# Gate and up products of the first two shared chunks issued in the attention's program, and the PSUM banks of the experts dealt out anew

## The chip, the cores and the metric

The kernel runs on one core of a Trainium2 chip. The metric is the device time of one execution in microseconds, lower is better. Engines are named as in the profile: PE is TensorE's matmuls, PEld its weight loads, DVE VectorE, ACT ScalarE, POOL GpSimd, SP SyncE.

## The reference, cut to what matters

`x` is 2 x 2048 tokens of width 256. Two residual steps, each behind a layer norm without weights:

```
x = x + attention(layernorm(x))
x = x + experts(layernorm(x))
```

The attention's scores are distances between three-dimensional positions of the tokens, the same for all 16 heads, under a causal mask, with softmax. The second step is what the change touches:

```
scores = softmax(xt @ gate_w.T);  idx = top_k(scores + gate_bias, 2)
y = sum over e of gate_e * (silu(xt @ w1[e].T) * (xt @ w3[e].T)) @ w2[e].T
z = (silu(xt @ sw1.T) * (xt @ sw3.T)) @ sw2.T
return y + z
```

There are eight experts with 256 hidden columns, of which two are taken for each token, and shared weights with 512 hidden columns that every token passes. All of it is float32.

## The kernel before, in words

A float32 product is done as three matmuls in a rounded format: both operands are split into a high part (a rounded copy, by ACT or POOL) and a low part (the difference, by DVE), and PE adds high x high, high x low and low x high in PSUM.

The kernel is two programs, one after the other, each a `Block` with an instruction stream for each engine. Both stand in a `with ExitStack() as ctx` (lines 133 and following for the first), and the instructions that a `Block` issues when it closes carry the line of that `with` (133) in the profile.

The first program does the attention for batch 0 and then batch 1. Its last part on PE are the value products of batch 1 (lines 1117 to 1121): for each block of 128 keys and 512 queries, E_hi and E_lo times VO, in the accumulators O_ps, which are banks 0 to 3 for the last quarter of the queries. Near the end PE also turns the normalised rows XN of token groups 0 and 1 (groups of 512 tokens) into banks 4 to 7 (N_ps, line 1105); ACT copies them to XT2_hi, DVE subtracts to get XT2_lo (`turned_lo`, line 905). DVE's order at the end is: the low parts of the last E blocks, between them the six pieces of the shared weights' low part (`shared_lo`, line 895), `turned_lo(0)`, then `finish` of the last four token tiles (reciprocal, scale and add into X, statistics: lines 812 to 820), with `turned_lo(1)` between the second and the third, and one last aggregation of statistics (line 636).

The second program does the shared experts for groups 0 to 5, then the routed experts in 71 slots of 128 token rows, then shared groups 6 and 7 and the sum. In each group there are four chunks n of 128 hidden columns. For a chunk PE does the 12 gate and 12 up matmuls (the function `products(n)`, 512 columns each, into G_ps[n % 2] and U_ps[n % 2], signalling s_g and s_u) and later the output products (`outputs(n)`, 12 of 256 columns, into Z_ps). In between, ACT applies silu to the gate (`sg`, line 1356), DVE multiplies by the up part (`hf`, line 1445, `hidden_whole`), ACT copies h_hi (line 1362), DVE subtracts h_lo (line 1449, `hidden_low`). PE's order by `shared(groups, ahead)` is: products of chunk n unless n stands in `ahead`, at n = 2 the counts (`counts()`, two matmuls on the choice), outputs of chunk n - 1. For groups 0 to 5 `ahead` is (0, 1), and `products(0)` and `products(1)` stand before the loop.

The order of DVE in the second program is written out by hand: the reciprocal and the choice of the two experts for batch 1 (lines 1471 to 1504), with `hidden_whole(0)`, `hidden_low(0)`, `hidden_whole(1)`, `hidden_low(1)` at fixed places within it, `hidden_whole(2)`, the places of the rows from the counts (`total`, `upto`, `hidden_low(2)` in it), and `slot` (line 1525). When the first `slot` is there, POOL begins to scatter the rows of X into `slots_in`, 64 indirect DMAs (line 1300), two for each tile of 128 tokens. SP's first instructions in the second program are the eight loads of the routed experts' weights W_raw; then it waits for all scatters, group by group, and loads the slots' rows (XS). DVE normalises them (line 1625), PE turns them (line 1745) and does the routed products.

All eight PSUM banks are dealt out by name in each program. In the second one, the shared chunks have T_ps, G_ps, U_ps, Z_ps, and the routed slots XT_ps, S_ps, HT_ps, Y_ps in the same pairs of banks.

Of the kernel before, what the change touches and what calls it, by code (L numbers as in the profile page):

```python
# [4 lines left out]
P = 128  # L5
# [5 lines left out]
KC = D // P  # L11
# [16 lines left out]
NS = 512  # L28
# [11 lines left out]
f32 = mybir.dt.float32  # L40
# [4 lines left out]
ALU = mybir.AluOpType  # L45
# [20 lines left out]
def attention_and_experts(nc, x, wv, bv, woT, bo, w3dT, b3d, gateT, gate_bias, wT, sw13T, sw2T, out):  # L66
# [6 lines left out]
    outer = ExitStack()  # L73
# [29 lines left out]
    sw13_hi = outer.enter_context(nc.sbuf_tensor("sw13_hi", [P, KC, 2 * NS], f32r))  # L103
# [27 lines left out]


    with ExitStack() as ctx:
        def sb(name, shape, dt=f32):
            return ctx.enter_context(nc.sbuf_tensor(name, shape, dt))

        def sem(name):
            return ctx.enter_context(nc.semaphore(name))
# [53 lines left out]

        bank = [ctx.enter_context(nc.psum_tensor(f"a_bank{i}", [P, 512], f32)) for i in range(8)]
        T_ps, V_ps = (bank[4:6], bank[6:8]), bank[0:4]
# [30 lines left out]
        s_w = [sem(f"s_w{k}") for k in range(2)]  # L225
        s_shi = sem("s_shi")
        s_gate = sem("s_gate")
        s_std0 = sem("s_std0")
# [79 lines left out]
        AHEAD = 3  # L308
# [294 lines left out]
        def _(dve):  # L603
# [90 lines left out]
            for b in range(NB):  # L694
# [197 lines left out]
                def shared_lo(w):  # L892
                    raw, hi, lo = shared_piece(w)
                    dve.wait_ge(s_shi, w + 1)
                    dve.tensor_tensor(lo, raw, hi.bitcast(f32), ALU.subtract)

# [5 lines left out]
                def turned_lo(G):  # L902
                    for c in range(KC):
                        dve.wait_ge(s_h0, KC * G + c + 1)
                        dve.tensor_tensor(XT2_lo[:, G, c, :], N_ps[KC * G + c][:, :],
                                          XT2_hi[:, G, c, :].bitcast(f32), ALU.subtract)

# [32 lines left out]
        def _(pe):  # L940
# [93 lines left out]
            for b in range(NB):  # L1034
# [60 lines left out]
                for n, (Q, kt) in enumerate(blocks):  # L1095
# [29 lines left out]
                    mm.then_inc(s_eb, 1)  # L1125

# [3 lines left out]
    with ExitStack() as ctx:  # L1132
# [53 lines left out]

        bank = [ctx.enter_context(nc.psum_tensor(f"bank{i}", [P, 512], f32)) for i in range(8)]
        C_ps = (bank[1][:, 0:NT * NX], bank[1][:, NT * NX:2 * NT * NX])
        T_ps, G_ps, U_ps, Z_ps = bank[0:2], bank[2:4], bank[4:6], bank[6:8]
        XT_ps, S_ps, HT_ps, Y_ps = bank[0:2], bank[2:4], bank[4:6], bank[6:8]  # L1190

# [6 lines left out]
        s_xtl = sem("f_xtl")  # L1198
        s_g = sem("f_g")
        s_u = sem("f_u")  # L1200
        s_sg = sem("f_sg")
# [455 lines left out]
        def _(pe):  # L1657
# [65 lines left out]
            pe.sem_inc(s_T, N_TURNED * KC)  # L1723
            products(0)
            products(1)
            shared(range(HALF), (0, 1))
# [90 lines left out]
```

## Time and profile before

| what | value |
|---|---|
| median of 3 runs | 562.71 us (562.35 to 562.73) |
| the profiled execution's own time | 565.71 us |
| span in that profile | 563.9 us |
| PE busy | 529.3 us, 94% |
| DVE busy | 428.5 us, 76% |
| ACT busy | 317.6 us, 56% |
| POOL busy | 265.1 us, 47% |
| mean granted clock of TensorE | 0.978 |

The span runs from the first to the last instruction of one execution. The page's chain is the work that ended last, followed back from the end; its shares say which engine set the time in each stretch. Timeline rows give an instruction's start and duration, and in brackets how long its engine had been idle and what released it. A matmul's duration holds its latency; the pace of a stream is the distance between starts. The granted clock is 1.00 at 2.4 GHz and 0.50 at 1.2 GHz.

### The profile page before, as it was taken

To read this page: it belongs to the slowest core of one execution; us is meant where nothing else is said; L and a number is where in the kernel's file an instruction comes from. 1 tells how busy PE (TensorE), PEld (TensorE's weight loads), DVE (VectorE), ACT (ScalarE), POOL (GpSimd) and SP (SyncE) were. 2 spreads that over 40 slices of the span, in tenths; PEclk is the share of its full clock that TensorE was granted. 3 is DMA by queue.
4 is the path that set the end of the run, shared out by engine and by line. 5 is a ranking of instruction groups with operands and counts; after the bars stand their busy time and mean duration, and the time that the engine had idled before them with its cause. 6 is when DMAs were issued, how large, how long until landed. Compare 5 with 4: busy or idle time off the path is not lost.

```text
span 563.9 us, 11301 instructions
## 1 busy us (share of the span) xinstructions
PE 529.3 (94%) x3362; PEld 468.3 (83%) x3362; DVE 428.5 (76%) x1169; ACT 317.6 (56%) x701; POOL 265.1 (47%) x580
## 2 busy tenths in 40 slices
PE   5989989999999996999999979999999999998984
PEld 5986889998679995888888868888888888887864
DVE  6789989687998997978667646667676666664896
ACT  2549999275997963344554325555555555554321
POOL 4057700073550000077777725777777676765000
PEclk9889999998999997999999979999999999999999
DMA  8999200000030003822222232333333333321995
GB/s 259 344 333 92 2 2 2 0 2 1 2 112 1 1 2 130 318 96 96 106 96 97 104 91 75 112 102 109 105 105 106 105 105 105 108 93 62 349 357 186
DMA packets 57402, 63.04 MB, mean 112 GB/s; under 512 B 15008, under 2 KB 50720, under 8 KB 57344
## 3 DMA queue, kind: packets, MB, share of 16 engines
q1 hardware_dynamic: 48944, 43.74, 27.2%
q0 software_dynamic: 6480, 17.90, 8.9%
q10 hardware_dynamic: 1920, 0.67, 0.5%
q8 instruction: 31, 0.51, 0.4%
q14 instruction: 27, 0.22, 0.1%
HBM read 30.65 MB, written 31.65 MB: 110 GB/s over the span
## 4 chain that ended last, share of the span: by engine, by line
PE 39%; POOL 12%; issue 5%; DVE 4%; DMA 1%; ACT 0%; DVEq 0%; SPq 0%; POOLq 0%
POOL slots_in L1300 12%; PE bank L1660 11%; PE bank L1662 11%; PE bank L1661 11%; PE bank L1745 3%; PE bank L1761 3%; DVE YG L1554 1%; DVE h_lo L1449 1%; DMA slots_in<-X,slot 0%; DVE hf L1445 0%; DMA XS<-slots_in 0%; PE bank L1669 0%; DVE X L1546 0%; DVE XN L1427 0%; DVE X L1568 0%
## 5 line engine op out<-in xcount | busy, mean ns | idle before, releaser
L1337 POOL DMA_INDIRECT token_out<-YS,to_row x71 | 71.9, 1012 | 48.7 <-DVE back L1629 44.8
L1300 POOL DMA_INDIRECT slots_in<-X,slot x64 | 67.6, 1057 | 37.1 <-issue 19.2
L1117 PE MATMUL a_bank<-VO,E_hi 128*128 128x266 f32 x272 | 78.8, 290 | 3.4 <-DVE E_lo L793 3.4
L1121 PE MATMUL a_bank<-VO,E_lo 128*128 128x266 f32 x272 | 77.6, 285 | 0.0
L1119 PE MATMUL a_bank<-VO,E_hi 128*128 128x264 f32 x272 | 77.6, 285 | 0.0
L1618 DVE TENSOR_TENSOR hr<-bank,sr 128x256 f32<-128x256 f32 x71 | 30.2, 425 | 61.8 <-ACT sr L1389 61.8
L1389 ACT ACTIVATE sr<-bank 128x256 f32<-128x256 f32 x71 | 27.3, 385 | 65.2 <-PE bank L1662 65.2
L1660 PE MATMUL bank<-W_hi,XST_hi 128*128 x142 | 62.7, 442 | 0.3 <-DVE XST_lo L1634 0.3
L1660 PE MATMUL bank<-XT_hi,sw_hi 128*128 128x512 f32 x128 | 51.8, 404 | 6.1 <-DVEq L1420 4.5
L1662 PE MATMUL bank<-W_hi,XST_lo 128*128 x142 | 57.4, 404 | 0.0
L1661 PE MATMUL bank<-W_lo,XST_hi 128*128 x142 | 57.0, 402 | 0.0
L1117 PEld LDWEIGHTS a_bank<-VO,E_hi 128*128 128x128 f32 x272 | 51.4, 189 | 4.8 <-DVE E_lo L793 4.6
L1362 ACT ACTIVATE h_hi<-hf 128x512 fp32r<-128x512 f32 x32 | 20.2, 632 | 58.6 <-DVE hf L1445 58.6
L1121 PEld LDWEIGHTS a_bank<-VO,E_lo 128*128 128x128 f32 x272 | 51.6, 190 | 0.0
L1119 PEld LDWEIGHTS a_bank<-VO,E_hi 128*128 128x128 f32 x272 | 51.4, 189 | 0.0
L793 DVE TENSOR_TENSOR E_lo<-E,E_hi 128x512 fp32r<-128x512 f32 (+1 forms) x80 | 47.2, 608 | 5.4 <-ACT E_hi L556 4.9
L1661 PE MATMUL bank<-XT_lo,sw_hi 128*128 128x512 f32 x128 | 51.0, 399 | 0.0
L1662 PE MATMUL bank<-XT_hi,sw_lo 128*128 128x512 f32 x128 | 50.7, 396 | 0.0
L1660 PE MATMUL bank<-W_hi,hT_hi 128*128 x142 | 45.4, 320 | 0.1
L1401 ACT ACTIVATE YS<-bank,by_weight 128x256 f32<-128x256 f32 x71 | 33.8, 476 | 19.5 <-PE bank L1662 19.5
L803 DVE TENSOR_SCALAR E<-a_bank 128x512 f32<-128x512 f32 (+3 forms) x80 | 43.3, 603 | 1.2 <-PE a_bank L1091 0.8
L1660 PE MATMUL bank<-sw_hi,h_hi 128*128 128x256 f32 x128 | 36.7, 287 | 6.2 <-DVE h_lo L1449 4.1
(269 smaller groups left out, 1605.9 us busy)
## 6 DMA issues: line engine op xcount, KB each, us to landing
XS<-slots_in SPq DMA_DIRECT2D x71, 131.0 KB, 2.1
slots_in<-blank SPq DMA_DIRECT2D x7, 1179.0 KB, 13.7
YG<-token_out SPq DMA_DIRECT2D x16, 512.0 KB, 8.9
W_raw<-in_wT_dram SPq DMA_DIRECT2D x8, 768.0 KB, 9.3
X<-in_x_dram SPq DMA_DIRECT2D x8, 512.0 KB, 8.4
out_dram<-X SPq DMA_DIRECT2D x32, 128.0 KB, 2.7
token_out<-YS,to_row POOLq DMA_INDIRECT x71, 2.5
slots_in<-blank SPq DMA_DIRECT2D x1, 1048.0 KB, 13.5
```

The source lines that it names most:

```text
L793: dve.tensor_tensor(E_lo[:, n % NE, 0:w], blk, E_hi[:, n % NE, 0:w].bitcast(f32), ALU.subtract).then_inc(s_el, 1)
L803: dve.tensor_scalar(blk, Q_ps[n % NQ][:, 0:w], 0.0, None, ALU.max).then_inc(s_e2, 1)
L1117: pe.matmul(O_ps[Q % 2][j][:, 0:XW + 2], E_hi[:, n % NE, cols], VO[:, kt, 0:XW + 2], start=(kt == 0), stop=False)
L1119: pe.matmul(O_ps[Q % 2][j][:, 0:XW], E_hi[:, n % NE, cols], VO[:, kt, XW + 2:VW], start=False, stop=False)
L1121: mm = pe.matmul(O_ps[Q % 2][j][:, 0:XW + 2], E_lo[:, n % NE, cols], VO[:, kt, 0:XW + 2], start=False, stop=(kt == qt))
L1300: pool.indirect_dma_start(out=xs, out_offset=bass.IndirectOffsetOnAxis(ap=slot[k][:, t:t + 1], axis=0), in_=X[:, t, 0:RW], in_offset=None) ...
L1337: pool.indirect_dma_start(out=ys, out_offset=bass.IndirectOffsetOnAxis(ap=to_row[:, i:i + 1], axis=0), in_=YS[:, i % NYS, :], in_offset=No ...
L1401: act.activation(YS[:, i % NYS, :], Y_ps[v][:, 0:D], ACT.Copy, scale=by_weight[:, i:i + 1])\
L1618: dve.tensor_tensor(hr[:, v, :], S_ps[v][:, D:2 * D], sr[:, v, :], ALU.mult).then_inc(s_hr, 1)
L1660: pe.matmul(out, a_hi, b_hi, start=start, stop=False, **kw)
L1661: pe.matmul(out, a_hi, b_lo, start=False, stop=False, **kw)
L1662: return pe.matmul(out, a_lo, b_hi, start=False, stop=stop, **kw)
```

## The change

PSUM banks and the semaphores s_g and s_u are allocated once for both programs. The 24 matmuls that `products(0)` and `products(1)` issued at the start of the second program are issued at the end of PE's stream in the first one, behind the last value product, with the same operands in the same order, and into banks 4, 6 (chunk 0) and 5, 7 (chunk 1). They wait for two new signals of DVE: the six low pieces of the shared weights (s_slo) and the four XT2_lo (s_l0). In the second program G_ps and U_ps are now banks 4-5 and 6-7 and Z_ps is 2-3; for the routed slots Y_ps is 2-3 and S_ps is 6-7.

```diff
--- before.py
+++ after.py
@@ -130,6 +130,10 @@
 
 
 
+    bank = [outer.enter_context(nc.psum_tensor(f"bank{i}", [P, 512], f32)) for i in range(8)]
+    s_g = outer.enter_context(nc.semaphore("f_g"))
+    s_u = outer.enter_context(nc.semaphore("f_u"))
+
     with ExitStack() as ctx:
         def sb(name, shape, dt=f32):
             return ctx.enter_context(nc.sbuf_tensor(name, shape, dt))
@@ -190,7 +194,6 @@
         E_hi = sb("E_hi", [P, NE, 512], f32r)
         E_lo = sb("E_lo", [P, NE, 512], f32r)
 
-        bank = [ctx.enter_context(nc.psum_tensor(f"a_bank{i}", [P, 512], f32)) for i in range(8)]
         T_ps, V_ps = (bank[4:6], bank[6:8]), bank[0:4]
         M_ps = bank[0:2]
         c_ps, g_ps, reach_ps = bank[6][:, 0:D], bank[6][:, D:XW], bank[6][:, XW:XW + 3]
@@ -224,6 +227,8 @@
         s_lgc = sem("s_lgc")
         s_w = [sem(f"s_w{k}") for k in range(2)]
         s_shi = sem("s_shi")
+        s_slo = sem("s_slo")
+        s_l0 = sem("s_l0")
         s_gate = sem("s_gate")
         s_std0 = sem("s_std0")
         s_rstd0 = sem("s_rstd0")
@@ -892,7 +897,7 @@
                 def shared_lo(w):
                     raw, hi, lo = shared_piece(w)
                     dve.wait_ge(s_shi, w + 1)
-                    dve.tensor_tensor(lo, raw, hi.bitcast(f32), ALU.subtract)
+                    dve.tensor_tensor(lo, raw, hi.bitcast(f32), ALU.subtract).then_inc(s_slo, 1)
 
                 def group_xn(G):
                     for t in range(G * GT, G * GT + GT):
@@ -903,7 +908,7 @@
                     for c in range(KC):
                         dve.wait_ge(s_h0, KC * G + c + 1)
                         dve.tensor_tensor(XT2_lo[:, G, c, :], N_ps[KC * G + c][:, :],
-                                          XT2_hi[:, G, c, :].bitcast(f32), ALU.subtract)
+                                          XT2_hi[:, G, c, :].bitcast(f32), ALU.subtract).then_inc(s_l0, 1)
 
                 dve.wait_ge(s_lgc, b + 1)
                 for n, (Q, kt) in enumerate(blocks):
@@ -1124,6 +1129,18 @@
                             mm.then_inc(s_acc, 1)
                     mm.then_inc(s_eb, 1)
 
+            pe.wait_ge(s_slo, 2 * AHEAD)
+            pe.wait_ge(s_l0, 2 * KC)
+            for n in range(2):
+                for w, bk, s_ready in ((0, bank[4:6], s_g), (NS, bank[6:8], s_u)):
+                    rows = slice(w + n * P, w + (n + 1) * P)
+                    for c in range(KC):
+                        hi, lo = sw13_hi[:, c, rows], sw13_lo[:, c, rows]
+                        pe.matmul(bk[n][:, :], hi, XT2_hi[:, 0, c, :], start=(c == 0), stop=False)
+                        pe.matmul(bk[n][:, :], hi, XT2_lo[:, 0, c, :], start=False, stop=False)
+                        mm = pe.matmul(bk[n][:, :], lo, XT2_hi[:, 0, c, :], start=False, stop=(c == KC - 1))
+                    mm.then_inc(s_ready, 1)
+
 
 
 
@@ -1184,10 +1201,9 @@
         sb("W_rest", [P, 2 * KC * NX * 3 * D - NT * TOPK * D])
         ZT.append(sb("ZT1", [P, GT, D]))
 
-        bank = [ctx.enter_context(nc.psum_tensor(f"bank{i}", [P, 512], f32)) for i in range(8)]
         C_ps = (bank[1][:, 0:NT * NX], bank[1][:, NT * NX:2 * NT * NX])
-        T_ps, G_ps, U_ps, Z_ps = bank[0:2], bank[2:4], bank[4:6], bank[6:8]
-        XT_ps, S_ps, HT_ps, Y_ps = bank[0:2], bank[2:4], bank[4:6], bank[6:8]
+        T_ps, Z_ps, G_ps, U_ps = bank[0:2], bank[2:4], bank[4:6], bank[6:8]
+        XT_ps, Y_ps, HT_ps, S_ps = bank[0:2], bank[2:4], bank[4:6], bank[6:8]
 
         s_home = sem("f_home")
         s_std = sem("f_std")
@@ -1196,8 +1212,6 @@
         s_T = sem("f_T")
         s_xth = sem("f_xth")
         s_xtl = sem("f_xtl")
-        s_g = sem("f_g")
-        s_u = sem("f_u")
         s_sg = sem("f_sg")
         s_hf = sem("f_hf")
         s_hh = sem("f_hh")
@@ -1721,8 +1735,6 @@
                 pe.matmul(C_ps[1], ones_b[:, :], rhs, start=True, stop=True).then_inc(s_cnt, 1)
 
             pe.sem_inc(s_T, N_TURNED * KC)
-            products(0)
-            products(1)
             shared(range(HALF), (0, 1))
             pe.wait_ge(s_slot, 3)
             pe.wait_ge(s_wrl, KC * NX)
```

## Rows read from the trace of the kernel before

**Rows 1.** the page's chain that ended last, its shares of the span by line.

```profile
POOL slots_in L1300 12%; PE bank L1660 11%; PE bank L1662 11%; PE bank L1661 11%; PE bank L1745 3%; PE bank L1761 3%; DVE YG L1554 1%; DVE h_lo L1449 1%; DMA slots_in<-X,slot 0%; DVE hf L1445 0%; DMA XS<-slots_in 0%; PE bank L1669 0%; DVE X L1546 0%; DVE XN L1427 0%; DVE X L1568 0%
```

**Rows 2.** timeline of POOL: start us, us, engine, line, operation, [idle before <-releaser].

```profile
239.05 1.17 POOL L1300 DMA_INDIRECT slots_in<-X,slot  x1 [17.90 <-DVE slot L1525]
...
324.93 0.97 POOL L1300 DMA_INDIRECT slots_in<-X,slot  x1 [0.30 <-issue]
```

**Rows 3.** one window: bounds, us, busy PE, PEld, DVE, ACT, POOL, clock, DMA, GB/s.

```profile
260.00:300.00 40.00, 40.00 (x239) 35.33 (x238) 29.16 (x46) 20.46 (x33) 31.01 (x30) 1.00 0.29 102
```

**Rows 4.** timeline of DVE at the end of the scatters.

```profile
327.67 1.40 DVE L1568 TENSOR_TENSOR X<-X,bank 128x512 f32<-128x512 f32 x2 [1.07 <-PE bank L1662]
329.74 0.41 DVE L1625 TENSOR_SCALAR XSN<-XS 128x256 f32<-128x256 f32 x1 [0.68 <-DMA XS<-slots_in]
```

**Rows 5.** timeline of SP at the start of the second program.

```profile
219.51 5.06 SPq L1267 DMA_DIRECT2D W_raw<-in_wT_dram  x8
```

**Rows 6.** timeline of PE from the last value product on.

```profile
214.90 0.28 PE L1121 MATMUL a_bank<-VO,E_lo 128*128 128x266 f32 x1
219.70 0.77 PE L1660 MATMUL bank<-XT_hi,sw_hi 128*128 128x512 f32 x1 [4.52 <-DVEq L1420]
...
221.12 0.63 PE L1660 MATMUL bank<-XT_hi,sw_hi 128*128 128x512 f32 x1
...
224.11 0.63 PE L1661 MATMUL bank<-XT_lo,sw_hi 128*128 128x512 f32 x1
...
225.06 0.39 PE L1661 MATMUL bank<-XT_lo,sw_hi 128*128 128x512 f32 x1
...
227.33 0.39 PE L1662 MATMUL bank<-XT_hi,sw_lo 128*128 128x512 f32 x1
227.56 0.28 PE L1660 MATMUL bank<-sw_hi,h_hi 128*128 128x256 f32 x1
...
245.42 0.36 PE L1660 MATMUL bank<-sw_hi,h_hi 128*128 128x256 f32 x1 [0.54 <-DVE ZT L1563]
```

**Rows 7.** instructions of line 133 by queue: duration min/median/max ns, first and last start.

```profile
L133 PEldq DRAIN  x1: 2422/2422/2422, 212.8 to 212.8; - x1
L133 DVEq DRAIN  x1: 220/220/220, 219.1 to 219.1; - x1
...
L133 PEldq EVENT_SEMAPHORE  x1: 51/51/51, 219.4 to 219.4; - x1
```

**Rows 8.** timeline of DVE across the end of the first program.

```profile
215.60 1.27 DVE L905 TENSOR_TENSOR XT_lo<-a_bank,XT_hi 128x512 fp32r<-128x512 f32 x2
...
219.04 0.18 DVE L636 BATCH_NORM_AGGREGATE mv<-st 128x2 f32<-128x6 f32 x1
...
223.37 0.29 DVE L1484 TENSOR_TENSOR tmp<-biased,red 128x128 f32<-128x128 f32 x1
225.13 0.69 DVE L1445 TENSOR_TENSOR hf<-bank,sg 128x512 f32<-128x512 f32 x1 [1.47 <-PE bank L1662]
...
226.70 0.69 DVE L1449 TENSOR_TENSOR h_lo<-hf,h_hi 128x512 fp32r<-128x512 f32 x1
...
232.30 0.19 DVE L1504 TENSOR_TENSOR X<-X 128x16 f32<-128x16 f32 x1
232.53 0.69 DVE L1445 TENSOR_TENSOR hf<-bank,sg 128x512 f32<-128x512 f32 x1
```

**Rows 9.** windows of half a microsecond, columns as in rows 3.

```profile
217.50:218.00 0.50, 0.00 (x0) 0.00 (x0) 0.49 (x3) 0.00 (x0) 0.00 (x0) 0.83 0.00 0
...
330.50:331.00 0.50, 0.43 (x3) 0.23 (x2) 0.46 (x3) 0.26 (x1) 0.35 (x3) 0.50 0.45 153
```

**Rows 10.** timeline of ACT in the second program.

```profile
221.71 1.28 ACT L1356 ACT_TABLE_LOAD   x1
223.00 0.60 ACT L1356 ACTIVATE sg<-bank 128x512 f32<-128x512 f32 x1
```

**Rows 11.** timeline of PE at the first expert slot.

```profile
330.21 1.25 PE L1745 MATMUL bank<-ident,XSN 128*128 128x128 f32 x4 [1.87 <-DVE XSN L1625]
```

## The prediction

> **What bounds the kernel now.** First the chain that ended last [rows 1]. Its largest single item is not a TensorE line but POOL's scatter of token rows, 12% of the span; TensorE's lines share the rest. Then POOL's own rows [rows 2]: the first of the 64 scatters starts at 239.05, released by `slot` from DVE after 17.90 us of waiting, and the last starts at 324.93, one after the other in between. So the stage from 239 to 326 has a length of its own, and everything before it is worth what it does to 239.05. Then the windows [rows 3]: TensorE is busy 40.00 of 40 us beside the scatters. Both chains end together: DVE's last sum of shared outputs runs 327.67 to 329.07, and the first slot's rows wait 0.68 us more for the DMA, to 329.74 [rows 4]. TensorE thus has 0.7 us of slack against the scatters, not more.
>
> What leads to 239.05 is the choice of experts of batch 1, on DVE. It begins in the second program, and the second program begins on all engines at once: SP, which waits for no semaphore there, issues its loads of W_raw at 219.51, and PE starts at 219.70 though it had done nothing since 215.18 [rows 5, 6]. The rows of the `with` line 133 say why [rows 7]: each engine ends the first program with a DRAIN, and all are released by one event at 219.4. PE's DRAIN starts at 212.8 and takes 2422 ns, to 215.2, which is the end of its last value product (214.90 + 0.28 [rows 6]): it lasts until the matmuls are through. DVE's comes last, at 219.1. So the release is at present set by DVE's last statistics (219.04 + 0.18 = 219.22 [rows 8]), and SP's first issue is 0.29 us behind that.
>
> **The change, part by part.**
>
> *Moved: 24 matmuls to before the release.* They wait for the four XT2_lo; the last two take 1.27 us from 215.60, to 216.87 [rows 8]; the six sw_lo pieces are earlier in DVE's order. With 0.1 us for the signal they start at 216.95, after an idle stretch of 1.8 us on PE. The granted clock fell at 217.8, some 2.6 us behind PE's last matmul (the mean of 0.83 over 217.5 to 218.0 puts it at 217.83) [rows 9]; at 216.95 it still stands at full speed. Pace at full clock: from 225.06 to 227.33 are ten steps, 0.227 us each; at half clock from 221.12 to 224.11 seven, 0.427 each [rows 6]. I take full clock: 24 x 0.227 = 5.45, and 0.16 for the tail of the last (0.39 - 0.227): PE ends at 222.56. All at half clock it would be 10.4 us, 227.3.
>
> *The wait that this adds.* PE's DRAIN now ends at 222.56, later than DVE's 219.28, so PE releases the barrier. With the same 0.29 us: 222.85 in place of 219.51, **+3.3 us** for everything in the second program: ACT's square root and table loads, DVE's choice, SP's eight loads, POOL's columns. Nothing of the choice's arithmetic can lie beside the moved products, since it stands behind the release.
>
> *Removed: the wait of the choice for products of chunk 0.* DVE had the choice's first part done at 223.37 + 0.29 = 223.66 and `hf` of chunk 0 started at 225.13, 1.47 us idle, released by PE [rows 8]. Now both banks are full at the release. ACT's silu is then the next late thing: its table load ends at 222.99 and `sg` runs 223.00 to 223.60 [rows 10]; both it and DVE's 223.66 shift by 3.3, so `hf` starts at 227.05, **-1.4 us**, net +1.9 against 225.13. From there to the end of the choice (232.30 + 0.19 = 232.49) DVE had no idle time, so it would reach `hf` of chunk 2 at 234.4.
>
> *Next late: products of chunk 2.* In PE's order these stand behind the output products of chunk 0, which need h_lo of chunk 0: 226.70 + 0.69 [rows 8] + 1.9 = 229.3. PE thus idles from 222.6 to 229.3 where before it had its 24 matmuls, and this idle stretch, 6.7 us, is long enough to lose the clock (4.5 us were). The output products have half the columns, so 12 x 0.213 (estimate, half of 0.427) = 2.6, to 231.9. Before, the pace changed 4.9 us after PE's restart (219.70 to about 224.6 [rows 6]); here that is 234.2. Of the 12 matmuls of chunk 2, 5.5 run slow until then and 6.5 fast: 2.3 + 1.5 + 0.2 tail, to 235.9. `hf` of chunk 2 starts at 236.0 against 232.53: **+3.5 us**; 1.6 us of DVE idle has come in place of the 1.47 removed. Bounds: if PE were at full clock there (229.3 + 1.4 + 2.7 + 0.2 = 233.6) DVE's 234.4 would decide, +1.9; all slow, 229.3 + 2.6 + 5.1 + 0.2 = 237.2, +4.7. I take the middle since the restart seen here is the nearest row.
>
> *After it.* From `hf` of chunk 2 to the first scatter are 6.52 us of DVE (232.53 to 239.05) with no wait for PE in them but the counts, which PE issues right behind those products as before. First scatter at 242.5, +3.5. PE goes on with the outputs of chunk 1 and chunk 3 some 4 us later than before; it had waited 0.54 us for the ZT copies at 245.42 [rows 6], which shift with DVE by 3.5, so PE falls back into step there. Both chains reach the experts +3.5 us late.
>
> *Banks, semaphores.* The new assignment moves G to 4-5, U to 6-7 and Z to 2-3, in both the shared chunks and the experts (S with U's, Y with Z's, HT with G's banks). It adds no instruction, and each first user of a bank still comes behind the last reader by the waits that stand (`hf`, `zf`, `hr`, `ys`); the counts' bank 1 is unchanged. Zero; if one such wait did bite, it would be once per transition, bounded by PE's idle stretch at that transition, 1.87 us at 330.21 [rows 11]. The signals added to ten DVE instructions cost nothing: the instruction behind each starts without it. SP's eight loads start 3.3 us later and their first reader, ACT's copy in chunk 4, is 3.5 later. Zero.
>
> A rule of the Trainium skill ("TensorE: Matmul & The Clock Gate", section "Back-to-back issue gap") speaks against the price of the moved work: a sustained stream of pairs of weight load and matmul with 512 columns would run at about 131 ns each. This trace has 227 ns for that very form at full clock, so the row decides; by the page the 24 would take 3.1 us.
>
> **Sum.** Release +3.3, wait at chunk 0 -1.4, wait at chunk 2 +1.6: +3.5 us. The profiled execution took 565.71 (span 563.9 and 1.8 around it), so it would become 569.2. The median of the runs, 562.71, lies 3.0 below the profiled one; the same sum on it gives **566.2 us**, 0.6% slower.
>
> **Rivals.**
> - *The clock falls during the moved products (slower still).* For it: after 1.87 us of idle at 328.3 to 330.2, about the gap expected here, the clock was at half by 330.5 though PE had started again [rows 9, 11]. Against: the matmuls behind that gap were narrow transposes, here they are of 512 columns. A stretch at half clock as long as that behind 219.70, 4.9 us, holds 11 of the 24 and adds 11 x 0.2 = 2.2 us: 568.4. Chance 0.18.
> - *The release is not held by PE and PE keeps its clock (faster).* The place is PE's DRAIN: if it passed while matmuls are in flight, the release stays at 219.5, `hf` of chunk 0 starts at 223.7 and the gain of 1.4 us reaches the scatters if chunk 2's products are on time: 561.3. It decides only if both hold; with the slow restart, chunk 2 ends at 232.5 again and nothing is gained. The 2422 ns of PE's DRAIN in rows 7 speak against it. 0.04.
> - *The loss is absorbed.* The same with the slow restart (562.8), or slack in front of the first scatter that I don't see. POOL's 17.90 us wait ends with `slot`, so against. 0.05.
> - *The page's pace.* Release only 1.0 us later; the chain behind it moves to +1.2, 563.9, by the same steps with 131 ns in the moved products alone. The row of 227 ns leaves it 0.02.
> - *My mechanism with its sizes*: 0.71, of itself 564.6 to 567.4, by the bounds +1.9 and +4.7.
>
> **Numbers.** Predicted 566.2. Range 564.2 to 568.8: it takes both bounds of the mechanism and the fall of the clock, with 0.4 for the spread of the runs. A measurement here tells 0.2%, 1.1 us, from no change: faster 0.04, within 0.06, slower 0.90.
>
> **What would show it.** In the changed profile: 24 PE rows of the moved line from about 217.0 to 222.6 at 0.23 us spacing; PE's DRAIN of line 133 ending with them and the event at 222.8 instead of 219.4; SP's W_raw at 222.8; no idle time of DVE before the first `hf`, about 1.6 before the third, released by PE; the first scatter at 242.5. Wrong in the release: the event stays near 219.4. Wrong in the clock: spacing of 0.43 within the 24, or a quick restart at 229 with `hf` of chunk 2 near 234.4. Wrong in the bound: a later first scatter with the experts' start not later by as much.

## The result and the profile after

The changed kernel takes 568.67 us, the median of 4 runs (567.68 to 569.44), against 562.72 before (median of 4 runs, 562.35 to 562.78): 5.95 us slower, ratio 1.0099, 95% interval [1.0073, 1.0125]. The profiled execution took 568.82 us, 3.11 above the profiled one of before, with a span of 567.1, 3.2 above.

PE first (start us, us, engine, line, operation, what released it). The 24 moved matmuls run at the full-clock pace, the first starting at 216.97 and the last at 222.31; then PE stands still until 229.49:

```profile
214.87 0.28 PE L1126 MATMUL bank<-VO,E_lo 128*128 128x266 f32 x1
216.97 0.47 PE L1139 MATMUL bank<-XT_hi,sw_hi 128*128 128x512 f32 x1 [1.82 <-DVE XT_lo L910]
...
222.31 0.39 PE L1141 MATMUL bank<-XT_hi,sw_lo 128*128 128x512 f32 x1
229.49 0.58 PE L1674 MATMUL bank<-sw_hi,h_hi 128*128 128x256 f32 x1 [6.79 <-DVE h_lo L1463]
...
230.09 0.41 PE L1676 MATMUL bank<-sw_hi,h_lo 128*128 128x256 f32 x1
230.30 0.41 PE L1674 MATMUL bank<-sw_hi,h_hi 128*128 128x256 f32 x1
...
233.07 0.63 PE L1676 MATMUL bank<-XT_hi,sw_lo 128*128 128x512 f32 x1
233.50 0.52 PE L1674 MATMUL bank<-XT_hi,sw_hi 128*128 128x512 f32 x1
233.85 0.40 PE L1675 MATMUL bank<-XT_lo,sw_hi 128*128 128x512 f32 x1
...
235.47 0.39 PE L1676 MATMUL bank<-XT_hi,sw_lo 128*128 128x512 f32 x1
```

The spacing is 0.21 us for 256 columns behind 229.49 and 0.43 for 512; between 233.50 and 233.85 it drops towards the full-clock pace, and the products of chunk 2 end with the one at 235.47. This answers [rows 6]. The line of the first program's `with` is now 137. Its DRAINs by queue (duration min/median/max ns, first and last start): PE's starts at 218.5 and takes 4288 ns, to 222.8, while DVE's is over at 219.2. This answers [rows 7]:

```profile
L137 PEldq DRAIN  x1: 4288/4288/4288, 218.5 to 218.5; - x1
L137 DVEq DRAIN  x1: 220/220/220, 219.0 to 219.0; - x1
```

SP's first issue of the second program follows at 222.98 instead of 219.51 [rows 5]:

```profile
222.98 4.97 SPq L1281 DMA_DIRECT2D W_raw<-in_wT_dram  x8
```

DVE, against [rows 8]: its statistics end at 219.17 (before: 219.22). The 1.47 us of idle time at the first `hf` are gone, and 1.54 us stand in front of the third, released by PE. `h_lo` of chunk 0, for which PE's outputs wait, is at 228.74:

```profile
218.99 0.18 DVE L641 BATCH_NORM_AGGREGATE mv<-st 128x2 f32<-128x6 f32 x1
...
226.85 0.29 DVE L1498 TENSOR_TENSOR tmp<-biased,red 128x128 f32<-128x128 f32 x1
227.17 0.69 DVE L1459 TENSOR_TENSOR hf<-bank,sg 128x512 f32<-128x512 f32 x1
...
228.74 0.69 DVE L1463 TENSOR_TENSOR h_lo<-hf,h_hi 128x512 fp32r<-128x512 f32 x1
...
234.32 0.20 DVE L1518 TENSOR_TENSOR X<-X 128x16 f32<-128x16 f32 x1
236.06 0.69 DVE L1459 TENSOR_TENSOR hf<-bank,sg 128x512 f32<-128x512 f32 x1 [1.54 <-PE bank L1676]
```

POOL's first and last scatter, against [rows 2]: 242.58 instead of 239.05, the last 3.94 us later:

```profile
242.58 1.17 POOL L1314 DMA_INDIRECT slots_in<-X,slot  x1 [17.96 <-DVE slot L1539]
...
328.87 0.96 POOL L1314 DMA_INDIRECT slots_in<-X,slot  x1 [0.30 <-issue]
```

At the first expert slot PE is idle for 2.12 us, and the clock falls at 336.2 (windows: bounds, us, busy PE, PEld, DVE, ACT, POOL, clock, DMA share, GB/s). This answers [rows 9, 11]:

```profile
334.43 1.00 PE L1757 MATMUL bank<-ident,XSN 128*128 128x128 f32 x4 [2.12 <-DVE XSN L1639]
```

```profile
227.00:233.00 6.00, 3.51 (x14) 3.39 (x15) 5.62 (x16) 1.81 (x4) 0.00 (x0) 0.50 1.03 408
...
332.00:336.00 4.00, 1.30 (x8) 0.63 (x7) 2.91 (x11) 0.77 (x2) 1.08 (x7) 1.00 0.51 134
336.20:339.50 3.30, 3.30 (x10) 2.55 (x9) 0.90 (x4) 0.77 (x2) 0.70 (x5) 0.50 0.46 122
```

A table from such rows of all traces that can be read to their end serves the rest; each kernel in it is described with its experiment below. "Release" is SP's first issue of W_raw; "slots" is the start of PE's first transposes ("turns") of slot rows, "group 6" that of its transposes of that group's rows behind the last slot, "end" the span. The last four columns are the differences: release to first scatter, first scatter to slots, slots to group 6, group 6 to the end.

| kernel | release | first scatter | slots | group 6 | end | to scatter | to slots | slot stage | last stage |
|---|---|---|---|---|---|---|---|---|---|
| before | 219.51 | 239.05 | 330.21 | 515.94 | 563.9 | 19.54 | 91.16 | 185.73 | 48.0 |
| b_again | 219.46 | 238.32 | 329.50 | 512.56 | 561.5 | 18.86 | 91.18 | 183.06 | 48.9 |
| banks | 218.85 | 237.56 | 328.68 | 511.73 | 560.7 | 18.71 | 91.12 | 183.05 | 49.0 |
| after | 222.98 | 242.58 | 334.43 | 518.89 | 567.1 | 19.60 | 91.85 | 184.46 | 48.2 |
| a_third | 222.81 | 242.16 | 333.77 | 518.49 | 566.9 | 19.35 | 91.61 | 184.72 | 48.4 |
| gate0 | 218.82 | 236.92 | 328.31 | 511.57 | 560.7 | 18.10 | 91.39 | 183.26 | 49.1 |
| chunk0 | 218.59 | 237.81 | 329.26 | 514.01 | 562.2 | 19.22 | 91.45 | 184.75 | 48.1 |
| warm12_2 | 222.49 | 240.59 | 331.87 | 514.88 | 563.7 | 18.10 | 91.28 | 183.01 | 48.8 |
| fill7 | 223.00 | 242.22 | 333.74 | 516.75 | 566.7 | 19.22 | 91.52 | 183.01 | 50.0 |
| gate0_fill | 219.98 | 238.07 | 329.38 | 512.62 | 562.8 | 18.09 | 91.31 | 183.24 | 50.2 |

Beside a_again, delay, warm1 and warm12, which ran together, every kernel took 617 to 640 us, the one before included (632.82), and in their four traces the time is lost between 250 and 400 us, so only the stretch up to the first scatter is read there: a_again has 19.52 us from release to scatter, as the change has elsewhere (19.60 and 19.35).

### The profile page after: what moved, and what is told of

Read it like the earlier page. It is cut to its first block, busy times and chain, and to the rows that moved or that the text cites. A ratio compares the mean times of both kernels' runs of the same rounds, so it can differ in the third digit from the quotient of the medians.

```text
span 567.1 us, 11302 instructions
## 1 busy us (share of the span) xinstructions
PE 527.3 (93%) x3362; PEld 468.1 (83%) x3362; DVE 428.6 (76%) x1169; ACT 317.4 (56%) x701; POOL 264.9 (47%) x580
## 4 chain that ended last, share of the span: by engine, by line
PE 38%; POOL 12%; issue 5%; DVE 4%; DMA 1%; ACT 1%; DVEq 0%; ACTq 0%; SPq 0%; POOLq 0%
POOL slots_in L1314 12%; PE bank L1674 11%; PE bank L1675 11%; PE bank L1676 11%; PE bank L1757 3%; PE bank L1773 3%; DVE YG L1568 1%; DMA slots_in<-X,slot 1%; DVE h_lo L1463 0%; DMA XS<-slots_in 0%; PE bank L1683 0%; DVE X L1560 0%; DVE hf L1459 0%; DVE XN L1441 0%; DVE X L1582 0%
## 5 line engine op out<-in xcount | busy, mean ns | idle before, releaser
L1351 POOL DMA_INDIRECT token_out<-YS,to_row x71 | 71.7, 1010 | 48.8 <-DVE back L1643 44.9
L1122 PE MATMUL bank<-VO,E_hi 128*128 128x266 f32 x272 | 78.7, 289 | 3.6 <-DVE E_lo L798 3.6
L1126 PE MATMUL bank<-VO,E_lo 128*128 128x266 f32 x272 | 77.7, 286 | 0.0
L1124 PE MATMUL bank<-VO,E_hi 128*128 128x264 f32 x272 | 77.6, 285 | 0.0
L1122 PEld LDWEIGHTS bank<-VO,E_hi 128*128 128x128 f32 x272 | 51.4, 189 | 4.8 <-DVE E_lo L798 4.7
L1126 PEld LDWEIGHTS bank<-VO,E_lo 128*128 128x128 f32 x272 | 51.6, 190 | 0.0
L1124 PEld LDWEIGHTS bank<-VO,E_hi 128*128 128x128 f32 x272 | 51.5, 189 | 0.0
L1674 PE MATMUL bank<-XT_hi,sw_hi 128*128 128x512 f32 x120 | 47.9, 399 | 1.6 <-issue 1.6
L1675 PE MATMUL bank<-XT_lo,sw_hi 128*128 128x512 f32 x120 | 47.2, 394 | 0.0
L1676 PE MATMUL bank<-XT_hi,sw_lo 128*128 128x512 f32 x120 | 47.0, 392 | 0.0
L808 DVE TENSOR_SCALAR E<-bank 128x512 f32<-128x512 f32 (+3 forms) x80 | 43.3, 601 | 1.3 <-PE bank L1096 0.9
```

The source lines that it names most:

```text
L808: dve.tensor_scalar(blk, Q_ps[n % NQ][:, 0:w], 0.0, None, ALU.max).then_inc(s_e2, 1)
L1122: pe.matmul(O_ps[Q % 2][j][:, 0:XW + 2], E_hi[:, n % NE, cols], VO[:, kt, 0:XW + 2], start=(kt == 0), stop=False)
L1124: pe.matmul(O_ps[Q % 2][j][:, 0:XW], E_hi[:, n % NE, cols], VO[:, kt, XW + 2:VW], start=False, stop=False)
L1126: mm = pe.matmul(O_ps[Q % 2][j][:, 0:XW + 2], E_lo[:, n % NE, cols], VO[:, kt, 0:XW + 2], start=False, stop=(kt == qt))
L1351: pool.indirect_dma_start(out=ys, out_offset=bass.IndirectOffsetOnAxis(ap=to_row[:, i:i + 1], axis=0), in_=YS[:, i % NYS, :], in_offset=No ...
L1674: pe.matmul(out, a_hi, b_hi, start=start, stop=False, **kw)
```

## The experiments

**b_again: the kernel before, a second time.** No edit.

> The kernel before, unchanged, for a second trace of it. The changed kernel was 5.95 us slower by the medians (568.67 against 562.72) and only 3.1 by the two profiled executions (568.82 against 565.71), since the profiled execution of before lay 3.0 above its own runs. Theory A (the profiled one of before was an unusual execution): this one's profile comes out near 562.7 and shows, against the first trace, a stretch that is about 3 us shorter; by the prediction's mechanism I look for it between PE's last value product at 214.9 and the first scatter. Theory B (a profile as such costs 3 us): it is again near 565.7.

Measured: 563.12 us median of 10 (562.75 to 568.67), beside it 31 runs of before from 560.5 to 566.26 with a median of 563.18; ratio 1.0015 [0.9985, 1.0045]. The profiled one took 563.23. Theory A (the first profiled execution was an unusual one) holds, but the 2.4 us of span lie only in part where I looked for them. DVE's first and third `hf` are at 224.40 and 231.79, 0.7 earlier than in the first trace:

```profile
224.40 0.69 DVE L1445 TENSOR_TENSOR hf<-bank,sg 128x512 f32<-128x512 f32 x1 [0.77 <-PE bank L1662]
...
231.79 0.69 DVE L1445 TENSOR_TENSOR hf<-bank,sg 128x512 f32<-128x512 f32 x1
```

The windows say why: PE restarts at half clock, but is back at full clock by 223.5, and at the first slot, where the clock fell in the first trace at 330.5, it stays at full.

```profile
219.80:223.00 3.20, 3.20 (x8) 2.53 (x9) 2.28 (x8) 3.14 (x6) 0.48 (x3) 0.50 0.69 247
223.50:231.00 7.50, 7.50 (x40) 6.16 (x38) 6.29 (x19) 2.41 (x5) 0.00 (x0) 1.00 1.03 405
326.00:333.00 7.00, 4.56 (x26) 3.54 (x27) 3.92 (x13) 1.10 (x4) 1.98 (x12) 1.00 0.40 112
333.00:340.00 7.00, 7.00 (x44) 5.97 (x43) 5.50 (x20) 3.61 (x12) 2.17 (x9) 1.00 0.19 51
```

In the table, the first trace against b_again: 0.7 us more to the first scatter, 2.7 more in the slot stage, 1.0 less in the last stage. The last is the clock too: the last output products, behind 2.42 us of idle time in both, start 0.12 us apart in the first trace and 0.21 apart in b_again, where the clock fell in them. So the execution on which the prediction's sum was made was one with an unusual share of half clock (mean 0.978; most executions of before have 0.984 to 0.987 and take 562.3 to 563.9).

**banks: only the new assignment of the banks.** The moved block issues nothing (its list `MOVED` is empty) and its two waits are out; `products(0)` and `products(1)` are back in the second program.

```diff
+MOVED = ()
...
-            pe.wait_ge(s_slo, 2 * AHEAD)
-            pe.wait_ge(s_l0, 2 * KC)
...
+                    if (n, w) not in MOVED:
+                        continue
...
             pe.sem_inc(s_T, N_TURNED * KC)
+            products(0)
+            products(1)
             shared(range(HALF), (0, 1))
```

> Only the new assignment of the banks; all 24 gate and up matmuls stand in the second program as before, and nothing waits for s_slo and s_l0. Theory A (banks cost nothing): 562.7, no change within 0.2%. Rival C (the 2.4 us that the prediction's sum lacks come from the new banks): 565.1.

Measured: 563.30 (562.49 to 565.93), ratio 1.0010 [0.9989, 1.0030]. Its four stages in the table are b_again's within 0.15 us; POOL's first scatter:

```profile
237.56 1.17 POOL L1315 DMA_INDIRECT slots_in<-X,slot  x1 [17.07 <-DVE slot L1540]
```

The banks cost nothing that can be measured (the interval ends 0.3% above no change; rival C's 2.4 us would be 0.4%). Rival C is out.

**gate0: only the 6 gate matmuls of chunk 0 moved.**

```diff
+MOVED = ((0, 0),)
...
             for n in range(2):
                 for w, bk, s_ready in ((0, bank[4:6], s_g), (NS, bank[6:8], s_u)):
+                    if (n, w) not in MOVED:
+                        continue
```

and the reverse condition in `products`, with `products(0)` and `products(1)` back in the second program.

> Of the 24 matmuls only the 6 gate matmuls of chunk 0 are issued in the first program; new banks as in the change. Theory A (what costs is that PE releases the second program late): they end near 218.6, before DVE's last statistics at 219.2, so the release stays at 219.4 and SP's loads at 219.5; PE is idle only 1.2 us and stays at full clock, hf of chunk 0 starts at 223.7 instead of 225.1. Then 561.3 if chunk 2's products are on time, 562.7 if PE loses the clock before them; in any case not slower than before. Rival C (banks): 564 to 565. Rival D (any matmul behind the value products delays the release): slower by a us or more.

Measured: 563.70 (561.43 to 564.78), ratio 0.9998 [0.9973, 1.0023]. PE, SP and DVE of its trace:

```profile
216.33 0.47 PE L1142 MATMUL bank<-XT_hi,sw_hi 128*128 128x512 f32 x1 [1.84 <-DVE XT_lo L911]
...
217.55 0.39 PE L1144 MATMUL bank<-XT_hi,sw_lo 128*128 128x512 f32 x1
219.01 0.47 PE L1677 MATMUL bank<-XT_hi,sw_hi 128*128 128x512 f32 x1 [1.07 <-DVEq L1437]
```

```profile
218.82 5.00 SPq L1284 DMA_DIRECT2D W_raw<-in_wT_dram  x8
```

```profile
218.35 0.18 DVE L642 BATCH_NORM_AGGREGATE mv<-st 128x2 f32<-128x6 f32 x1
...
223.01 0.69 DVE L1462 TENSOR_TENSOR hf<-bank,sg 128x512 f32<-128x512 f32 x1
...
230.40 0.69 DVE L1462 TENSOR_TENSOR hf<-bank,sg 128x512 f32<-128x512 f32 x1
```

The 6 end at 217.94, before DVE's 218.53; from the first moved matmul to the release are 2.49 us, what DVE needs. The clock holds, and no `hf` waits: 18.10 us from release to scatter, against 18.71 in banks, 18.86 in b_again and 19.54 in the first trace of before. Rival D is out. But the runs did not become faster, and theory A's 561.3 to 562.7 is missed by 1 us: of ten, five took 561.4 to 563.2 and five 564.2 to 564.8. The one trace is of an execution of the first five (562.43), so where the others lost their time isn't known.

**chunk0: the 12 matmuls of chunk 0 moved.** As gate0, with `MOVED = ((0, 0), (0, 512))`.

> The 12 gate and up matmuls of chunk 0 are issued in the first program, those of chunk 1 at the start of the second; new banks. Theory A: PE's drain ends at 219.9, release 0.7 us later than before (SP's loads at 220.2), hf of chunk 0 at 224.4, 0.8 earlier than before; first scatter between 0.8 earlier and 0.7 later: 561.9 to 563.4, 2.7 us below the changed kernel's sum of the prediction and far below its 568.7. Rival C (banks) 565 or more.

Measured: 565.46 (563.89 to 568.77), ratio 1.0044 [1.0023, 1.0064]. PE, SP and the third `hf`:

```profile
215.31 0.47 PE L1142 MATMUL bank<-XT_hi,sw_hi 128*128 128x512 f32 x1 [1.83 <-DVE XT_lo L911]
...
217.92 0.39 PE L1144 MATMUL bank<-XT_hi,sw_lo 128*128 128x512 f32 x1
218.94 0.47 PE L1677 MATMUL bank<-XT_hi,sw_hi 128*128 128x512 f32 x1 [0.63 <-DVEq L1437]
...
225.10 0.39 PE L1677 MATMUL bank<-sw_hi,h_hi 128*128 128x256 f32 x1 [3.17 <-DVE h_lo L1466]
```

```profile
218.59 4.96 SPq L1284 DMA_DIRECT2D W_raw<-in_wT_dram  x8
```

```profile
231.29 0.69 DVE L1462 TENSOR_TENSOR hf<-bank,sg 128x512 f32<-128x512 f32 x1 [1.15 <-PE bank L1679]
```

From the first moved matmul to the release are 3.28 us, 0.79 more than in gate0 (0.7 was expected). (The first program itself ended 1.1 us earlier than gate0's, so the release at 218.59 can't be compared directly.) The idle stretch in front of the outputs of chunk 0 is 3.17 us, the clock falls at 225.5, and the third `hf` waits 1.15 us for PE. At the first expert slot the clock falls too, at 331.4 behind a gap of 1.71 us, and the slot stage takes 184.75 us. The median lies above the 561.9 to 563.4 that I gave, at rival C's 565 (which banks has excluded), and above its own trace (563.89, clock 0.986): six of the ten runs have a clock of 0.981 or 0.982 and take 565.2 to 565.8, two more 0.976 and 0.979 and 567.8 and 568.8. Where those executions lost the clock, the one trace doesn't show.

**a_again and a_third: the change, again.** No edit.

> The changed kernel, unchanged, for more runs and a second trace: the runs of one kernel spread by more than 2 us with the mean granted clock of the execution (the kernel before: 562.9 at 0.985, 565 at 0.98). Theory A (+3.5 by the release and the choice, the rest by TensorE clock lost at the expert slots' start): median 567 to 569; the release at 223.0 and the first scatter near 242.6 in each trace, the rest moving with the half-clock stretches. Rival E (the 5.95 was an accident of four executions): 565.5 to 566.5.

> The changed kernel once more, unchanged: on the chip of its second look every kernel, the one before too, took some 630 us, with stalls of all engines between 250 and 400 us, so that only the stretch up to the first scatter could be read there. Theory A: 567 to 569 beside 562.9, release to first scatter 19.5 us as in both traces so far. Rival E (the 5.95 was an accident of four executions): 565.5 to 566.5.

Measured: a_again 629.26 (616.92 to 630.15), beside 632.82 of before (see above), so its expected median can't be tested; release 222.97, first scatter 242.49. a_third 568.85 (568.29 to 569.12) beside 563.22 of before, ratio 1.0098 [1.0073, 1.0123]. The 5.95 was no accident; rival E is out. Its four runs and the four of the first result lie within 1.8 us at a clock of 0.979 or 0.980.

**delay: the late release without its benefit.** The moved matmuls signal nothing and all products are issued again in the second program.

```diff
                         mm = pe.matmul(bk[n][:, :], lo, XT2_hi[:, 0, c, :], start=False, stop=(c == KC - 1))
-                    mm.then_inc(s_ready, 1)
...
             pe.sem_inc(s_T, N_TURNED * KC)
+            products(0)
+            products(1)
             shared(range(HALF), (0, 1))
```

> The 24 matmuls are issued at the end of the first program as in the change, but signal nothing, and all of products(0) and products(1) are issued again in the second program: the change's late release without its benefit, at 24 more matmuls. Theory A: release at 223.0 again; PE goes on at once and at full clock, hf of chunk 0 still at 227.2 (behind silu), no idle stretch in front of outputs(0) but 0.6 us, products of chunk 2 by 233.8, third hf at 234.5, first scatter at 241.1: 2.7 above the second trace of before, 1.5 below the change. 565.7 to 567.2 by the runs, so faster than the change although it does more work. Rival F (moving the products away is what helps and the release is cheap): slower than the change, 570 or more, since 5.4 us of PE work come back.

Measured: 633.56 us beside 632.82 of before, ratio 1.003 [0.998, 1.008], and beside 629.26 of the change (a_again), where all took some 630. That delay would be faster than the change is thus not shown by the times, and rival F, which is about the whole, not refuted by them. The trace can be read up to the scatter. PE and the third `hf`:

```profile
217.63 0.47 PE L1139 MATMUL bank<-XT_hi,sw_hi 128*128 128x512 f32 x1 [1.84 <-DVE XT_lo L910]
...
223.77 0.47 PE L1673 MATMUL bank<-XT_hi,sw_hi 128*128 128x512 f32 x1 [0.45 <-DVEq L1433]
...
230.09 0.39 PE L1673 MATMUL bank<-sw_hi,h_hi 128*128 128x256 f32 x1 [0.60 <-DVE h_lo L1462]
230.31 0.28 PE L1674 MATMUL bank<-sw_lo,h_hi 128*128 128x256 f32 x1
```

```profile
235.15 0.69 DVE L1458 TENSOR_TENSOR hf<-bank,sg 128x512 f32<-128x512 f32 x1
```

From the first matmul of the first program's end to the release are 5.9 us, as in the change (6.0). PE goes on at full clock, idle only 0.60 us before the outputs, which take 0.28 us each instead of 0.41; the third `hf` waits for nothing, and release to scatter is 18.11 us, 1.2 to 1.5 less than in the three traces of the change, with 24 matmuls more. Up to the scatter both halves of the mechanism are shown: the release costs what PE still has to do, and what the moved matmuls leave behind is an idle stretch that costs 1.2 to 1.5 us.

**warm1: the idle stretch behind the release filled.**

```diff
+            def keep_awake(count):
+                for _ in range(count):
+                    pe.matmul(T_ps[0][:, :], sw13_hi[:, 0, 0:P], XT_hi[:, 0, 0, :], start=True, stop=True)
+
             pe.sem_inc(s_T, N_TURNED * KC)
+            keep_awake(26)
             shared(range(HALF), (0, 1))
```

> The changed kernel with 26 unused matmuls (512 columns, into the free bank 0) at the head of PE's second program, in the idle stretch between the release and outputs(0). Theory A (1.5 us of the loss is TensorE at half clock behind that idle stretch): outputs(0) at 229.5 as before but at 0.12 us spacing, third hf at 234.5 released by nothing, first scatter at 241.1; 1.5 us faster than a_again. Rival G (clock irrelevant there, the choice on DVE sets it): same as a_again.

Measured: 634.84 us beside 632.82, ratio 1.003 [1.001, 1.006], and beside 629.26 of a_again, than which it was to be 1.5 faster; where all took some 630, the times can't test that. PE and the third `hf`:

```profile
223.64 6.17 PE L1739 MATMUL bank<-XT_hi,sw_hi 128*128 128x512 f32 x26 [0.48 <-PEq L137]
229.96 0.39 PE L1674 MATMUL bank<-sw_hi,h_hi 128*128 128x256 f32 x1
230.18 0.28 PE L1675 MATMUL bank<-sw_lo,h_hi 128*128 128x256 f32 x1
```

```profile
235.03 0.69 DVE L1459 TENSOR_TENSOR hf<-bank,sg 128x512 f32<-128x512 f32 x1
```

The outputs take 0.28 us each again, release to scatter 18.12 us. Counted from the release (223.44), theory A holds to the tenth up to the scatter; rival G is out.

**warm12 and warm12_2: the gap in front of the slots filled as well.**

```diff
+            keep_awake(7)
             pe.wait_ge(s_slot, 3)
             pe.wait_ge(s_wrl, KC * NX)
```

> warm1 and 7 more unused matmuls behind the last outputs of group 5, in front of the first expert slot, where PE is idle 2.1 us in the changed kernel and the clock fell afterwards in its trace. Theory A (the unexplained 2.4 us are mostly this fall, which the kernel before has in few of its executions): 1.4 to 2.7 us faster than warm1, 564.5 to 565.7, with no half-clock stretch between 330 and 345, and less spread. Rival H (the fall is no more frequent than before and the 2.4 us lie elsewhere): same as warm1.

> The changed kernel with 26 unused matmuls in the idle stretch behind the release and 7 in front of the first expert slot, again, for a time beside the change's on one chip. Seen already: release to first scatter 18.1 us with the 26. Theory A: 1.5 us by the first group and 1.4 to 2.7 by the second: 564.0 to 565.7, no half-clock stretch between 220 and 345, and so 1.3 to 3 above before: the late release (3.5) less the head start of the first hf. Rival H (the clock at the expert slots costs no more after the change than before): 566.5 to 567.5.

Measured: warm12 635.58 beside 632.82 (nothing of the slots can be read there; from its release, 225.96 behind a first program that ran 3 us longer, to the scatter are 18.10 us). warm12_2 565.80 (565.42 to 567.98) beside 563.22 of before, ratio 1.0045 [0.9998, 1.0093], and beside 568.85 of a_third on the same chip: 3.05 us less. That is 0.1 above theory A's range and 0.7 below rival H's, though two of the five runs took 567.1 and 568.0. PE at the first slot, with the filling in front:

```profile
329.75 1.78 PE L1739 MATMUL bank<-XT_hi,sw_hi 128*128 128x512 f32 x7
331.87 1.00 PE L1763 MATMUL bank<-ident,XSN 128*128 128x128 f32 x4 [0.34 <-DVE XSN L1639]
```

The slot stage is 183.01 instead of 184.72 and no half clock stands between 220 and 345. By the table the 3.2 us of span against a_third are 1.25 to the scatter, 0.33 to the slots, 1.71 in the slot stage, 0.32 from an earlier release, -0.4 in the last stage. So the clock in the slot stage is the largest part, which speaks against rival H.

**fill7: only the 7 in front of the slots.**

```diff
+            keep_awake(7)
             pe.wait_ge(s_slot, 3)
```

> The changed kernel with only the 7 unused matmuls in front of the first expert slot, none behind the release. Theory A: release 222.8, release to first scatter 19.4 as in the change, slot stage 183.0 instead of 184.5 to 184.7: 567.0 to 567.4, 1.6 us below the change's 568.7, and 4 above before, which is the late release with the first hf's gain and the new wait at the third. Rival I (the fall only moves to a later place, or the filling delays the first slot): 568.5 or more.

Measured: 568.66 (568.31 to 572.26) beside 563.45, ratio 1.0102 [1.0069, 1.0134]: no gain on the change. Theory A held for the stage and failed for the whole (567.0 to 567.4). The slot stage is 183.01, but the clock falls later, where the shared chunks of group 6 begin:

```profile
336.00:340.00 4.00, 4.00 (x21) 3.22 (x20) 2.41 (x9) 1.59 (x5) 1.08 (x7) 1.00 0.32 95
519.70:523.00 3.30, 3.30 (x9) 2.51 (x9) 0.00 (x0) 0.60 (x1) 0.00 (x0) 0.50 0.26 82
```

The last stage is 50.0 us instead of 48.2 to 48.4, which gives back what the slots had gained. That is rival I, the fall at a later place. But warm12_2 has the same 7 matmuls, and its clock stayed at full behind group 6 (last stage 48.8 us): whether the filling brings on the later fall is not shown.

**gate0_fill: the candidate.** gate0 with the same 7.

> The candidate for a faster kernel: only the 6 gate matmuls of chunk 0 in the first program (they end before DVE does, so the release isn't late), the new banks, and 7 unused matmuls in front of the first expert slot. Theory A: release as before, release to first scatter 18.1 us instead of 18.7 to 19.5, slot stage (first turn of slot rows to the turn of group 6) 183.0 us in every execution since the clock no longer falls at its start: 560.8 to 562.0, 1 to 2 below before, with fewer runs at 564 to 566 than gate0 had. Rival H (the fall there is not what separated gate0's runs at 562 from those at 564.5): median as gate0's, 563.7 beside 563.2.

Measured: 564.44 (561.51 to 566.35) beside 563.45, ratio 1.0012 [0.9993, 1.0031]. Not faster; theory A's 560.8 to 562.0 is missed, and the median is near rival H's 563.7. In its trace release to scatter is 18.09 and the slot stage 183.24, as expected, but the first program ran 1.2 us longer than gate0's, with a half-clock stretch near 134 us that gate0's lacks (release 219.98 against 218.82), the clock fell again at the start of group 6, and the last stage took 50.2. The trace also shows what no other does, the clock falling within the moved matmuls:

```profile
217.48 0.47 PE L1142 MATMUL bank<-XT_hi,sw_hi 128*128 128x512 f32 x1 [1.83 <-DVE XT_lo L911]
...
219.07 0.63 PE L1144 MATMUL bank<-XT_hi,sw_lo 128*128 128x512 f32 x1
```

The gap in front of them was 1.83 us, as in the others, and the last of the 6 starts 1.59 us behind the first instead of 1.22 (gate0). DVE ended no earlier than PE here (both DRAINs at 219.7), so the release did not suffer; with 24 moved matmuls it presumably would, which no run shows. No version beat the kernel before.

## Why the prediction was right, and where its size was off

*Release +3.3.* Measured +3.5 between the traces of before and after (219.51 to 222.98), PE's DRAIN ending with the moved matmuls. Their spacing was 0.23 as taken. The clock did not fall in them in any of the traces with 24 of them, so that rival did not occur there. It can happen, though: behind a gap of the same size the clock fell within the moved matmuls of gate0_fill, so that full clock in the eight traces with 24 is no certainty for every execution. gate0, chunk0 and delay show the rule: from the first moved matmul to the release 2.5 us with 6 matmuls (DVE decides), 3.3 with 12, 5.9 to 6.0 with 24. The rival that PE's DRAIN would not hold the release is out. The 131 ns that the Trainium skill gives for a matmul of 512 columns in a sustained stream of weight loads and matmuls ("TensorE: Matmul & The Clock Gate", "Back-to-back issue gap") are not what these traces show; 227 ns are.

*First `hf` -1.4, third +1.6.* Forecast 227.05 and 236.0, measured 227.17 and 236.06; the idle time removed was 1.47, the one added 1.54. delay and warm1 show that the cause of the added wait is the clock lost in PE's idle stretch. First scatter forecast 242.5, measured 242.58.

*Both chains reach the experts +3.5 late.* Measured +4.2 (330.21 to 334.43). The last scatter was 0.4 later than the first one's shift, and SP issued the load of the first slot's rows 0.3 later still behind it (331.85 instead of 327.63); from that issue to DVE's first row of the slots it took 2.11 us in both. In the table this stretch is 91.1 to 91.2 for the kernels that move nothing and 91.3 to 91.9 for the others. I did not find what lengthens it; it stays open.

*The sum on the profiled execution, 569.2.* Measured 568.8: +3.1 for +3.5. That it came so near is in part luck: by the table the 3.2 us of span are 3.5 release, 0.1 to the scatter, 0.7 to the slots, -1.3 in the slot stage, where the first trace of before had lost even more to half clock than the changed one did, and 0.2 in the last stage.

*The sum on the median, 566.2.* Measured 568.7. What was mis-sized is the step "the same sum on it": +3.5 on the median, where +5.95 was measured. It took the profiled execution of before for the median one with 3 us more in places that the change doesn't touch. In fact that execution lost 0.7 us to half clock at the restart of the second program and 2.7 us at the first slot, and 1.0 us less than b_again in the last stage. The usual execution, as b_again and banks show it, does not have the first two losses. The changed kernel has both kinds: in its trace the clock is at half for over 6 us from 227 on, and again at the first slot. So of the terms of the sum, the -1.4 at the first `hf` was too large for the usual execution: in b_again PE is back at full clock by 223.5, and DVE waits there for 0.77 us and not 1.47. Against b_again the 5.6 us of span are 3.5 release, 0.7 to the scatter, 0.7 to the slots, 1.4 in the slot stage, -0.7 in the last. The first two, 4.2, are the mechanism.

*The range, 564.2 to 568.8.* The median lies 0.13 below its top. That top was put there for a fall of the clock within the moved products, which did not come; the clock at the first slot, which did, was no term of the sum. That the range held is to that extent luck, while the mechanism up to the first scatter was right.

*Open.* Why the changed kernel loses the clock at the slots in both traces read there and before in one of two, with gaps of the same size (1.89 and 2.12 us against 1.87 and 1.86). It is not the 24 matmuls alone: chunk0 lost it there too, behind 1.71 us, while banks (1.79) and gate0 (2.08) did not. The place of the gap in time is a candidate, and in fill7 and gate0_fill the fall stands elsewhere; but no run here moved the gap alone. So the 1.4 us are located, not explained, and that they go back to the change is likely (its eight runs have a mean clock of 0.979 or 0.980, most of before 0.984 to 0.987) and not shown.

## What to carry to other kernels

Work moved ahead of an all-engine join is free only up to the moment at which the slowest engine arrives there. Here 6 matmuls fitted, with 0.6 us to spare; 12 held the join back by 0.8 us and 24 by 3.5, and with it a chain of DVE and POOL that had nothing to do with them. Ask what the move leaves behind: behind 3.17 and 6.79 us with nothing to do PE had lost its clock here, and the next products paid for it. And before adding a difference to the median, find out by a second trace whether the profiled execution is the usual one.

## What the runs showed of the hardware

TensorE's clock can be lost in or just behind a gap of under 2 us. At the first expert slot PE was idle 1.87 us in the first trace of before, 1.89 in a_third and 1.71 in chunk0, and the clock was then at half for some 7, 3 and 3 us; in b_again (1.86), banks (1.79) and gate0 (2.08) it stayed at full. The slot stage behind it took 185.7, 184.7 and 184.8 us with the fall and 183.1 to 183.3 without. The same holds for the gap of 1.8 us in front of the moved matmuls: full clock in ten traces, a fall in one (gate0_fill). Seven unused matmuls of 512 columns in the gap at the slots went with full clock there in all three traces that have them (183.0 to 183.2), without making the kernel faster by themselves.

PE's DRAIN at the end of a program lasts until its matmuls are through (4288 ns, to 222.8, where it waits for the 24 moved ones), and the other engines start their next program only then.

Runs of one unchanged kernel, the one before, spread from 560.5 to 568.7 us, with a mean granted clock from 0.989 down to 0.972. The clock is not all of it: at 0.984 there are runs of 562.1 and of 566.1 us. So a step of 1 us in one trace, such as gate0's, can't be told in the medians of ten runs.
